# Two side units per projection chunk, and the w1 and w2 loads of the FFN issued by ScalarE instead of GpSimd

## The reference

```
# x: (2, 8192, 2048), 16 heads, 128 "nope" + 64 "rope" dims for q and k, 128 for v
q = x @ Wq.T;  k = x @ Wk.T;  v = x @ Wv.T
q_rope, k_rope = rope(q_rope), rope(k_rope)
scores = q_nope.k_nope / sqrt(128) + q_rope.k_rope / sqrt(64)
x = layernorm(x + (softmax(scores) @ v) @ Wo.T)

def quantize(w):                      # gamma: one number for a whole matrix
    gamma = mean(abs(w))
    return clip(round(w / (gamma + 1e-8)), -1, 1)

# w1, w2: (5632, 2048), w3: (2048, 5632)
h = sigmoid(x @ quantize(w1).T) * (x @ quantize(w2).T)
x = layernorm(x + h @ quantize(w3).T)
```

## Time and profile before

| | us |
|---|---|
| median of 3 runs (slowest core) | 12688.69 |
| lowest and highest | 12636.33, 12898.49 |
| the profiled execution, its time | 12636.33 |
| span of its slowest core (core 7) | 12634.8 |
| span of its fastest core (core 3) | 12419.6 |
| P0, core 7 | 0 to about 4278 |
| P1 | to about 7950 |
| P3 | to about 8670 |
| P4, phases A of the two halves | 8670 to 9981, 10640 to 11970 |

### The profile page before, as it was taken

The page is one execution under the profiler, slowest core; times in us unless marked ns, Lnnn a source line. Parts: engine busy times, 40 slices in busy tenths (PEclk is TensorE's granted clock), DMA queues, the critical chain, the costliest instruction groups (busy, mean ns, idle before and its releaser), DMA issues.

```text
span 12634.8 us, 106433 instructions; the slowest of 8 cores (12419.6 to 12634.8 us)
## 1 busy us (share of the span) xinstructions
PE 8639.0 (68%) x34596; PEld 3351.6 (27%) x34596; DVE 4378.6 (35%) x4504; ACT 3942.5 (31%) x3777; POOL 779.4 (6%) x665
## 2 busy tenths in 40 slices
PE   6758668776674388888888888544565691555682
PEld 2223223332221133323333333211222230222231
DVE  2403314124013377777777777211111100111100
ACT  2002011120131366666666666102323101333200
POOL 0000000000000000000000000232000002000002
PEclk9879889888887699999999999777767785777785
DMA  7455365373443301010010110554222212222221
GB/s 140 96 99 130 85 121 110 74 136 87 97 111 94 97 13 39 26 39 13 26 39 13 31 35 4 73 80 95 70 70 70 80 57 93 67 73 73 73 74 60
DMA packets 833314, 904.53 MB, mean 72 GB/s; under 512 B 412672, under 2 KB 713728, under 8 KB 808960
## 3 DMA queue, kind: packets, MB, share of 16 engines
q0 software_dynamic: 471232, 356.54, 16.7%
q1 hardware_dynamic: 361536, 541.18, 13.7%
HBM read 908.07 MB, written 161.48 MB: 85 GB/s over the span
## 4 chain that ended last, share of the span: by engine, by line
PE 51%; ACT 15%; DMA 13%; DVE 8%; issue 4%; another core or an unknown queue 3%; POOL 3%; SPq 2%; ACTq 0%; DVEq 0%; POOLq 0%
PE pp L597 7%; PE pp L430 7%; PE pp L1128 7%; ACT arena L815 7%; PE pp L800 6%; PE pp L1133 5%; PE pp L1177 5%; PE pp L805 5%; DMA arena<-w3t 3%; DMA arena<-wvt 2%; PE pp L838 2%; PE pp L834 2%; DMA arena<-wot 2%; DMA arena<-y2scr 2%
## 5 line engine op out<-in xcount | busy, mean ns | idle before, releaser
L825 DVE TENSOR_TENSOR arena<-arena 128x1024 f32<-128x1024 f32 x2016 | 2470.4, 1225 | 528.5 <-ACT arena L815 429.6
L815 ACT ACTIVATE arena<-pp,arena 128x1024 bf16<-128x1024 f32 x2048 | 2283.9, 1115 | 899.7 <-PE pp L838 586.5
L430 PE MATMUL pp<-arena 128*128 128x512 bf16 x7680 | 1814.6, 393 | 349.9 <-DMA arena<-wkt 278.4
L1128 PE MATMUL pp<-arena 128*128 128x512 bf16 x2816 | 861.6, 474 | 1356.7 <-DVE arena L1113 1356.7
L800 PE MATMUL pp<-arena 128*128 128x512 bf16 x4096 | 1587.6, 388 | 282.7 <-ACT arena L815 113.1
L805 PE MATMUL pp<-arena 128*128 128x512 bf16 x4096 | 1590.5, 388 | 0.0
L597 PE MATMUL pp<-arena 128*128 128x512 bf16 x4096 | 919.6, 388 | 291.4 <-DMA arena<-wvt 291.4
L430 PEld LDWEIGHTS pp<-arena 128*128 128x128 bf16 x7680 | 740.9, 101 | 1347.5 <-issue 585.0
L317 DVE TENSOR_REDUCE arena<-arena 128x1 f32<-128x2816 f32 (+1 forms) x108 | 298.1, 2760 | 1539.1 <-DMA arena<-w3t 542.5
L1128 PEld LDWEIGHTS pp<-arena 128*128 128x128 bf16 x2816 | 321.1, 116 | 1886.2 <-issue 1779.4
L1177 PE MATMUL pp<-arena 128*128 128x512 bf16 x2816 | 751.1, 435 | 94.6 <-DMA arena<-w3qg 94.6
(11 more groups left out here) (124 smaller groups left out, 5151.6 us busy)
## 6 DMA issues: line engine op xcount, KB each, us to landing
arena<-w3t SPq DMA_DIRECT2D x88, 1024.0 KB, 5.6
arena<-w1t POOLq DMA_DIRECT2D x88, 1024.0 KB, 7.6
arena<-w2t POOLq DMA_DIRECT2D x88, 1024.0 KB, 9.8
arena<-wkt POOLq DMA_DIRECT2D x96, 512.0 KB, 10.0
kscr<-arena SPq DMA_DIRECT2D x384, 128.0 KB, 2.0
arena<-w1t SPq DMA_DIRECT2D x32, 1408.0 KB, 6.8
arena<-w2t SPq DMA_DIRECT2D x32, 1408.0 KB, 6.5
arena<-w3qg SPq DMA_DIRECT2D x32, 1408.0 KB, 13.8
```

The source lines that it names most:

```text
L430: self.op("tensor", lambda E, f=f, ps=ps, t=wk, lo=tok_lo, n=ntok: E.matmul(ps, t[:, f * 128:(f + 1) * 128], xh[:, f * 2048 + lo: f * 2048 ...
L815: self.op("scalar", lambda E, ps=psS, pt=ptile: E.activation(out=pt, in_=ps, func=AF.Exp, bias=self.negmh_bc, scale=1.0), waits=ew, inc="p ...
L825: self.op("vector", lambda E, pt=ptile: E.tensor_tensor(out=lacc, in0=lacc, in1=pt, op=ALU.add), waits=lw, inc="p1l")
L1128: self.op("tensor", lambda E, f=f, ps=psA, tc=tc, w1q=w1q: E.matmul(ps, w1q[:, f * 128:(f + 1) * 128], x1h[:, f * 1024 + tc * 512: f * 102 ...
```

## The change

Two edits to P0 and one to P4. In the nope chunks of the four k/v blocks and of the q block the call of `emit_side_unit()` is doubled. In phase A of the FFN the two loads of w1 and w2 stand in ScalarE's list instead of GpSimd's; their waits, buffers and semaphores are the same, and so is their place in the program: ahead of the four signs of their own chunk, behind the two sigmoids of the chunk before.

```diff
@@ -570,6 +570,7 @@
                 emit_nope_chunk(oc, d["wkt"], d["kscr"], v * 2048, False)
                 if SUB >= 5:
                     emit_side_unit()
+                    emit_side_unit()
             for g in range(4 if SUB >= 2 else 0):
                 emit_rope_pair(g, d["wkt"], d["kscr"], v * 2048, False)
@@ -1082,11 +1084,11 @@
-                self.op("gpsimd", lambda E, o=o: E.dma_start(
+                self.op("scalar", lambda E, o=o: E.dma_start(
                     out=w1f.rearrange("p (c o) -> p c o", c=16),
                     in_=d["w1t"][:, o * 128:(o + 1) * 128].rearrange("(c p) o -> p c o", p=128)),
                         waits=wA, inc="p4w", inc_amt=16)
-                self.op("gpsimd", lambda E, o=o: E.dma_start(
+                self.op("scalar", lambda E, o=o: E.dma_start(
                     out=w2f.rearrange("p (c o) -> p c o", c=16),
                     in_=d["w2t"][:, o * 128:(o + 1) * 128].rearrange("(c p) o -> p c o", p=128)),
                         inc="p4w", inc_amt=16)
```

## The result

The changed kernel is slower: 1.074 times the time of the kernel before, 95% interval 1.0688 to 1.0791, from 14 timed runs of each on one chip in turns. The medians over all runs are 13965.71 us (13581.44 to 14223.02) against 12793.48 us (12632.1 to 12991.11). The rows of the changed kernel are those of an execution with the full clock on all cores (but for some 30 us on four of them): 13549.62 us, where the lowest run of the kernel before on the same chip took 12421.39 us, with mean clocks (0.844 to 0.846) like those of a traced execution that has no stretch of the lower clock.

What follows compares the result with a forecast made beforehand. No engine was busy throughout; TensorE's largest idle time was in phase A's closed chain of sigmoid, quantizing and matmuls. 12636.3 + 279 (P0) + 857 (P4) = 13772, rounded 13770 us; range 13550 to 14050, with two rivals 13450 to 14150.

Steps and rivals of the forecast that it cites:

- mechanism of P4: FFN phase A: loads queued behind ScalarE's second sigmoid start late, first sign waits, transfer enters the closed chain; +857 us.
- The rival on the other side: Phase A: ScalarE's DMAs issue while its sigmoid still waits, so transfers stay hidden and P4 costs 0; 12895 us, chance 0.02.
- the start of the sum: Whole kernel: the profiled run's 12636.3 us, to which 279 for P0 and 857 for P4 were added.
- The rival "the clock comes back": Phase A: more idle time brings slow cores back to full clock, 2.3 us a chunk, -200, 13570 us; chance 0.15.
- P4's term: Phase A: the bare transfer of both loads costs 10.2 us a chunk in 86 of 88 chunks, +877 us.
- The -20 for the starts of the halves: Phase A, first chunk of each half: input lands 5 and 7 us sooner, quantizing saves another 2 and 6; -20 us.
- P0 was right term by term: P0: second units lengthen k/v blocks, units run out in block 3, q block and tail shorten; +279 us, bounds +120 to +440.
- the tail: End of P0: its 16 units at 12.7 us vanish, -203 us, leaving TensorE some 30 us of waiting at L777.
- the double gamma unit: P0 nope chunks: a second w1/w2 unit waits for the first's sum, period 28.9 us, +11.7 a chunk.
- the double w3 chunk: P0 block 2: two w3 units make a chunk 25.5 us, from 2 x 8.2 + 1 + 5.9 + 2.
- 16 x (23.9 - 15.6): P0's q block: 16 chunks lose their w3q units, period from 23.9 to 15.6 us, given as -131 us.

Runs made afterwards that it cites:

- the form with early loads on ScalarE: Kernel before with only the w1 and w2 loads moved to ScalarE, issued ahead of the chunk's two sigmoids; median 12882.11 us against 12937.6.
- P4's part alone: Kernel before with only the w1 and w2 loads moved from GpSimd to ScalarE, side units single; median 13673.26 us against 12937.6.
- the last kernel above: Kernel before with P0's side loads issued two units ahead, phase A's quantizing a chunk ahead, w1 and w2 loads waiting separately; median 11037.63 us, ratio 0.855.
- the two kernels with two buffers: Kernel before with two gamma buffers: doubled side units, 12740.62 us; or single calls, two per value part, loads two units ahead, 12099.83 us; before 12853.04.
- the late place on GpSimd: Kernel before with w1 and w2 loads kept on GpSimd but also waiting for the previous chunk's second sigmoid; median 13847.96 us against 12937.6.

## Why the prediction was right, and where its number was off

**The mechanism of P4 is shown.** Issue behind the sigmoid, the first sign waiting for w2 in all 88 chunks, the price gone with an earlier place on the same queue, and back with a late place on the other one. The rival on the other side (transfers issued while the sigmoid still waits) would have shown an issue 10 us ahead of the first sign's old place; w1's issue comes 0.02 us behind the sigmoid's start.

**The step that failed most is the start of the sum.** 279 + 857 was added to the time of core 7 in one execution, 12636.3. The earlier trace rows already showed that this core ran its matmuls in phase A at 4.38 us and core 0 at 3.62. Phases A and B took core 7 3942 us in all and core 3 3704, 238 less. At full clock the kernel before takes 12421.39 us, and 12421 + 1136 = 13557, 8 us from the 13549.62 measured. Where cores of one execution differ in clock, the sum belongs on the core at full clock, with the lower clock as a separate term.

**The rival "the clock comes back" gave 13570, and that is where the time at full clock lies, but not by its reason.** It wanted the longer pause per chunk to bring core 7 back to full clock. Against it: the kernel before has such executions too (12421.39, and the form with early loads on ScalarE 12456.63, whose pauses are no longer than before), and P4's part alone and the changed kernel, with the long pauses, also have executions with the lower clock. In one of the changed kernel, cores 0, 1, 6 and 7 take 1668 to 1703 us for a half of phase A and the others 1639 to 1653.

**Which cores have the lower clock when.** In every trace that has long stretches with 0.81 the pattern is one: of the four cores of a die, one pair has it from its first matmuls on and the other pair up to its last ones, for the same length. In the profiled execution of before, cores 2 and 3 have it from 75 to 1645 us of their span and cores 0 and 1 from 10750 to about 12310 (1570 and 1560 us); cores 4 and 5 from 75 to 3390 and cores 6 and 7 from 9072 to 12389 (3315 and 3317 us). In the last kernel above it is 6234 us on core 2 and on core 0, and 4133 and 4130 us on cores 4 and 6. Two pairs that start at different times, with the lower clock while both compute, would look like this, and the kernel would have no part in it. That is not shown, since the spans of a profile have no common time. The stretches do say that core 7 had the full clock in P0 and P1 and the lower one in phases A and B, so that 12636.3 is a sum of both.

**P4's term was 10.2 us, measured 9.5.** 815 / 86 = 9.48 by the stages (each half has 43 pauses inside its stage), 831.8 / 88 = 9.45 by the waits. The working put the transfer at the 260 GB/s of 512 B pieces plus 2.1 us; in the chunk shown the sign starts 9.36 us after w1's issue (9998.92 to 10008.28), 0.8 less than that, and 0.58 of it lies beside the sigmoid, because the issue follows the sigmoid's start and not its end. This is 62 us of the miss, toward the low end that was given (8.7 a chunk).

**The -20 for the starts of the halves** shows locally and not in the total. The half's input lands sooner, 15.6 us in the median against the 20.9 of the earlier trace rows:

```profile
DMA to landing us min/median/max: 13.3/15.6/17.8
```

From the issue of that load to the first matmul of phase A it was 21.9 and 28.5 us in the two halves (core 7, before) and is 13.5 and 17.9: 19 us less, as forecast. But TensorE's whole pause there fell only from 70.5 to 67.0 us in the first half, and grew from 229.2 to 249.3 in the second, where cores of the changed kernel's one execution differ by more than that (219 to 265 us). So it can't be counted on in the time.

**P0 was right term by term**, within 33 us: +204, +154, +257, +112, -210, -236 for +187, +151, +247, +127, -230, -203. The largest error is the tail. Of it I took away 16 units at 12.7 us and left some 30 us of waiting at L777. In the changed kernel that line, now L779, waits half as long:

```profile
PE pp L779 <- DVE arena L656: 15.3, 1, 15.3
```

So 220.7 of the 236.0 us of the earlier trace rows went; and the wait behind it, for keys from memory (L800, now L802), fell from 34.6 to 20.0 us, which the sum did not have. The other is the double gamma unit, 204 / 16 = 12.8 us in block 0 where the sum had 11.7; why was not tried. Two slips of the working are small beside that: the terms of the double w3 chunk add up to 25.3 and not 25.5, and 16 x (23.9 - 15.6) is 133 and not 131, 4 us together. That 281 meets 279 to 2 us is partly luck, since these errors cancel; the sign and rank of each block are not. Its reason, a load's landing in an in-order list behind one buffer, is borne out by the two kernels with two buffers.

**Together**, from 13772: the base was 215 too high (12636 for 12421), P4 62 too high, the start of the halves' -20 doesn't show in the time, P0 2 too low, and 33 us are left over: 13772 - 215 - 62 + 20 + 2 + 33 = 13550. The 33 us fit phase B, which takes this core 63 us more than core 3 before and 1217 to 1316 us over the cores of this execution; that they lie there is not shown, as the run of 12421.39 us has no trace.

## What to carry to other kernels

A DMA in a compute engine's in-order list starts no sooner than the instruction ahead of it: before moving a load to another engine, find what that engine waits for at that place, and if it is the end of the loop's own matmuls, the whole transfer becomes path (here 9.5 us, 86 times); the same issue placed before those waits costs nothing. A unit of side work with one buffer holds its engine for its landing time more than for its work. The first of a step may hide under what the other engines have in hand (16.9 us a chunk against 15.5 with no wait), and a second one then finds nothing left to hide under (30.7 us); the cure is the load of the next piece behind the reader of the one before (P0 from 4237 to 3538 us). When a chain is opened, look at once for the next one over the buffers (load, read, load), and do the sum on a core that has the full clock in the stage in question.

## What the runs showed of the hardware

- **Loads behind each other from ScalarE's queue come in sooner than from GpSimd's.** The same 2 x 1 MB in 512 B pieces, started bare in the chain, end the wait after 8.78 us (ScalarE's queue) and 11.60 us (GpSimd's); over phase A they cost 9.5 against 12.7 us a chunk. The medians over 88 chunks, issue to landing, are 5.7 and 9.1 us for w1 and w2 (P4's part alone) against 7.6 and 9.8 us (the late place on GpSimd). In the two chunks shown, 1.9 of the 2.8 us come from w2's later issue (1.72 us after the sigmoid's end against 0.17 before it) and 0.9 from the time between that issue and the sign (9.88 against 8.95). The Trainium skill (DMA: Bandwidth & Descriptors, section "Anatomy of one DMA — SWDGE (gpsimd) path") would give 6.8 us for this pair, an estimate by that page; the GpSimd rows, 11.02 us from w1's issue (9017.26) to the sign (9028.28), don't bear it out.
- **The second of two issues takes longer.** ScalarE's first load takes 0.38 us of the queue, the second, right behind it, 1.78 us, and 2.81 us in the early form (medians over 88 chunks 1.7 in both), where these 3.2 us lie beside matmuls and cost nothing that phase A's time shows.
- **Cores of one die have the lower clock in different stretches of their spans.** In the last kernel's profile cores 0 and 2, of one die, take 16.8 and 13.8 us a chunk of phase A, at 0.81 and 1.00 granted; cores 2 and 3 had their 0.81 in the first 6317 us instead, where P0 took them 3955 us and core 0 3562. In phase A that is 3.0 us of each chunk; in the kernel before, core 7 had 1.1 and 1.5 us a chunk more than core 3 in the two halves.
- **One of six runs of the last kernel took 18987.84 us**, with mean granted clocks of 0.53 to 0.71. No other run of any kernel here came near that, and this one has no trace; its cause is open.
